# Unit 0 of a feature-crossing kernel: every x_b block selected by matmuls from x_a, none loaded; d stored earlier on SP, passes reordered

## The reference

```python
for Wk, bk in zip([W0, W1, W2], [b0, b1, b2]):
    z = jnp.einsum('bid,bjd->bdij', base, curr)
    curr = jnp.einsum('bdij,ijh->bhd', z, Wk) + bk[None, :, None]
    logit.append(curr)
pooled = jnp.sum(jnp.concatenate(logit, axis=1), axis=-1)
out = pooled @ lin_w + lin_b
```

## Time and profile before

| | us |
|---|---|
| median of 3 runs | 180.6 (180.23 to 180.7) |
| the profiled execution, own time | 180.91 |
| its span (first to last instruction) | 179.1 |
| PE busy | 173.1 (97%) |
| DVE busy | 153.1 (85%) |
| ACT busy | 72.9 (41%) |
| POOL busy | 11.9 (7%) |

### The profile page before, as it was taken

One profiled execution on the slowest core, in us unless ns is written; L12 is line 12 of the kernel. 1 busy time (PEld: TensorE's weight loads), 2 busy tenths in 40 slices (PEclk: granted clock), 3 DMA queues, 4 the chain that ended last, 5 costly groups with the idle time before them and its releaser, 6 DMA issues.

```text
span 179.1 us, 2565 instructions
## 1 busy us (share of the span) xinstructions
PE 173.1 (97%) x800; PEld 118.0 (66%) x800; DVE 153.1 (85%) x141; ACT 72.9 (41%) x80; POOL 11.9 (7%) x20
## 2 busy tenths in 40 slices
PE   6799998999999999999999999999999999999995
PEld 1264665767777777777777777777777777777772
DVE  0799966299999999999999999999999999995012
ACT  2554900064643364426442654255424641450020
POOL 3251804000000000000000000000000000000000
DMA  5999844999879577847794778577857760000000
GB/s 159 400 413 399 268 111 115 407 419 408 264 236 328 140 231 231 327 141 231 231 328 138 225 232 264 188 220 226 284 171 225 232 202 0 0 0 4 0 0 0
DMA packets 12668, 37.59 MB, mean 210 GB/s; under 512 B 2548, under 2 KB 3668, under 8 KB 12660
## 3 DMA queue, kind: packets, MB, share of 16 engines
q1 hardware_dynamic: 11408, 36.39, 61.2%
q10 hardware_dynamic: 1252, 1.09, 2.3%
HBM read 36.40 MB, written 1.07 MB: 209 GB/s over the span
## 4 chain that ended last, share of the span: by engine, by line
PE 85%; DMA 6%; DVE 4%; SPq 2%; issue 1%; ACT 0%; DVEq 0%
PE q_ps L497 42%; PE c_ps L497 39%; DMA x_a<-xa 3%; DVE xb_z L262 2%; DMA pair_sb<-d_dram 1%; SPq L172 1%; DMA d_dram<-w_d 1%; PE q_ps L562 1%; PE q_ps L506 1%; PE c_ps L541 1%; SPq L166 1%; PE c_ps L636 1%; PE q_ps L541 1%; PE c_ps L640 0%; DVE w_post L283 0%
## 5 line engine op out<-in xcount | busy, mean ns | idle before, releaser
L366 ACT ACTIVATE z_high<-xb_z 126x1024 fp32r<-126x1024 f32 x56 | 59.2, 1061 | 81.6 <-DVE xb_z L262 77.6
L269 DVE TENSOR_TENSOR z_low<-xb_z,z_high 126x1024 fp32r<-126x1024 f32 x56 | 68.7, 1231 | 0.5 <-ACT z_high L366 0.4
L262 DVE TENSOR_TENSOR xb_z<-x_a,xb_z 126x1024 f32<-126x1024 f32 x50 | 61.3, 1226 | 3.7 <-DMA xb_z<-xw 3.7
L497 PE MATMUL c_ps<-z_high,wc_high 126*101 126x512 f32 x112 | 35.4, 397 | 0.3 <-DVE z_low L269 0.3
L497 PE MATMUL c_ps<-z_high,wc_low 126*101 126x512 f32 x112 | 35.0, 394 | 0.0
L497 PE MATMUL c_ps<-z_low,wc_high 126*101 126x512 f32 x112 | 35.0, 394 | 0.0
L497 PE MATMUL q_ps<-z_high,wq_high 126*101 126x512 f32 x108 | 34.0, 396 | 0.9 <-DVE wq_low L312 0.9
L497 PE MATMUL q_ps<-z_high,wq_low 126*101 126x512 f32 x108 | 33.8, 394 | 0.0
L497 PE MATMUL q_ps<-z_low,wq_high 126*101 126x512 f32 x108 | 33.7, 393 | 0.0
L497 PEld LDWEIGHTS c_ps<-z_high,wc_high 126*101 126x101 f32 x112 | 18.2, 165 | 8.8 <-ACT z_high L366 1.0
L497 PEld LDWEIGHTS c_ps<-z_high,wc_low 126*101 126x101 f32 x112 | 18.5, 165 | 7.5
(11 more groups left out here) (58 smaller groups left out, 61.5 us busy)
## 6 DMA issues: line engine op xcount, KB each, us to landing
xb_z<-xw SPq DMA_DIRECT2D x50, 512.0 KB, 4.4
x_a<-xa SPq DMA_DIRECT2D x7, 512.0 KB, 5.1
w_post<-w1x SPq DMA_DIRECT2D x4, 512.0 KB, 8.7
w_d<-w2h SPq DMA_DIRECT2D x4, 404.0 KB, 6.3
pair_sb<-w_pairs SPq DMA_DIRECT2D x3, 202.0 KB, 9.9
xb_z<-xw ACTq DMA_DIRECT2D x2, 256.0 KB, 4.6
x_a<-xa SPq DMA_DIRECT2D x2, 256.0 KB, 4.7
d_dram<-w_d SPq DMA_DIRECT2D x2, 189.4 KB, 3.7
```

Source lines behind the costliest of these rows:

```text
L262: nc.vector.tensor_tensor(xb_z[0:K, c, :], x_a[0:K, u % 2, :], x_b, ALU.mult).then_inc(z_done, 1)
L269: nc.vector.tensor_tensor(z_low[0:K, m % SLOTS, :], xb_z[0:K, c, :], z_high[0:K, m % SLOTS, :].bitcast(fp32), ALU.subtract).then_inc(low_d ...
L366: nc.scalar.activation(z_high[0:K, m % SLOTS, :], xb_z[0:K, m % C, :], ACT.Copy).then_inc(high_done, 1)
L497: last = nc.tensor.matmul(ps[0:J, h * B:(h + 1) * B], w[0:K, c * J:(c + 1) * J], z[0:K, slot, h * B:(h + 1) * B], start=(c == 0 and k == 0 ...
```

## The change

`SELECTED` is 6: chunk 6 is selected as well, and chunk 0 by two selections of half the columns (`select_first`, `form_first`), so no x_b of unit 0 is loaded: the two 256 KB loads on ACT's queue and SP's last load (512 KB) go. Chunk 0's selection goes to `c1_ps[0]`; the order of the first instructions on PE, DVE and ACT is written anew; the warm-up loop runs 10 times, not 14. Two of the ten stores of d move from ACT to SP, one from SP to ACT. In `c1_chunk` and `q_chunk` the pass with the low weights is last, and the waits for `z_low` and for the low weights stand right ahead of the passes that use them.

```diff
-SELECTED = 5
+SELECTED = 6
-WARM = 14
+WARM = 10
-        sel_ps = (q_ps[0], c1_ps[1])
+        sel_ps = (c1_ps[0],) + (c1_ps[1], q_ps[0]) * (SELECTED // 2 + 1)
...
@@ sync: stores of d
             store_d(sp, 1, LEFT + UPPER_AT[0], 0, 2 * GI, (DR - DB, DR))
+            store_d(sp, 0, LEFT + F, 0, RIGHT, (32, DR))
+            store_d(sp, 1, LEFT - 2 * GI, 0, 2 * GI, (0, 32))
             sp.wait_ge(dgroup_copied_dve, 1)
             store_d(sp, 0, LEFT + 2 * GI, 2 * GI, GI, (0, DB))
             store_d(sp, 1, LEFT + UPPER_AT[2], 2 * GI, GI, (DR - DB, DR))
-            store_d(sp, 1, 0, 3 * GI - (LEFT - 2 * GI), LEFT - 2 * GI, (0, 32))
...
@@ vector
-            form_first(0, xa_first, xb_first)
             split_x(0)
-            form_first(1, xa_loaded[0], xb_loaded[0]).then_inc(z_done, 1)
             split_x(1)
-            split(0, 0)
+            form_first(0).then_inc(formed_first, 1)
+            form_first(1).then_inc(z_done, 1)
             form(0, 1)
             form(0, 2)
+            split(0, 0)
+            form(0, 3)
             split(0, 1)
+            form(0, 4)
             split(0, 2)
-            form(0, 3)
-            form(0, 4)
-            form(0, 5)
             copy_d(2)
             split(0, 3)
+            form(0, 5)
+            split(0, 4)
             form(0, 6)
-            for m in range(4, C):
-                split(0, m)
+            split(0, 5)
+            split(0, 6)
...
@@ scalar
-            load_first_xb(0, xb_first)
-            load_first_xb(1, xb_loaded[0])
...
+            act.wait_ge(formed_first, 1)
             round_high(0, 0)
             cast_w0(0)
+            act.wait_ge(const_done, 1)
+            nc.scalar.activation(const_sb[:, :], const_ps, ...).then_inc(const_copied, 1)
             round_high(0, 1)
-            round_high(0, 2)
             act.wait_ge(v_multiplied, 1)
             nc.scalar.activation(v_rows[:, :], v_ps, ACT.Copy).then_inc(v_rows_copied, 1)
-            act.wait_ge(const_done, 1)
+            round_high(0, 2)
...
-            act.wait_ge(dgroup_copied, 3)
-            store_d(act, 0, LEFT + F, 0, RIGHT, (32, DR))
-            store_d(act, 1, LEFT - 2 * GI, 0, 2 * GI, (0, 32))
             round_high(0, 3)
             copy_d(3)
+            act.wait_ge(dgroup_copied_dve, 1)
+            store_d(act, 1, 0, 3 * GI - (LEFT - 2 * GI), LEFT - 2 * GI, (0, 32))
+            round_high(0, 4)
             cast_w0(2)
             cast_w0(3)
...
@@ tensor
+            def chunk_pass(ps, w, z, m, first, last):
+                c, slot = m % C, m % SLOTS
+                for h in range(2):
+                    end = nc.tensor.matmul(ps[0:J, h * B:(h + 1) * B], w[0:K, c * J:(c + 1) * J],
+                                           z[0:K, slot, h * B:(h + 1) * B],
+                                           start=(c == 0 and first), stop=(c == C - 1 and last))
+                return end
...
             def c1_chunk(it, m):
...
+                chunk_pass(c1_ps[u % 2], wc_high, z_high, m, True, False)
+                pe.wait_ge(low_done, it * BODY + (m + 1))
+                chunk_pass(c1_ps[u % 2], wc_high, z_low, m, False, False)
+                if m in WC_CUTS[:-1]:
+                    pe.wait_ge(wc_ready, WC_CUTS.index(m) + 1)
+                last = chunk_pass(c1_ps[u % 2], wc_low, z_high, m, False, True)
...
             def q_chunk(it, m):
                 if m in PREP_CUTS[:2]:
+                    pe.wait_ge(wq_highs, PREP_CUTS.index(m) + 1)
...
+                chunk_pass(q_ps[u % 2], wq_high, z_high, m, True, False)
+                chunk_pass(q_ps[u % 2], wq_high, z_low, m, False, False)
...
-            c1_chunk(0, 0)
...
+            turn_v()
             c1_chunk(0, 0)
...
             d_group(3)
-            for m in range(1, C):
+            c1_chunk(0, 1)
+            select_xb(6)
+            for m in range(2, C):
                 c1_chunk(0, m)
```

More of the change, by code:

```diff
@@ L491, in _ @@
         def _(pe):
-            def chunk_products(ps, high, low, m):
+            def chunk_pass(ps, w, z, m, first, last):
                 c, slot = m % C, m % SLOTS
-                for k, (w, z) in enumerate(((high, z_high), (low, z_high), (high, z_low))):
-                    for h in range(2):
-                        last = nc.tensor.matmul(ps[0:J, h * B:(h + 1) * B], w[0:K, c * J:(c + 1) * J],
-                                                z[0:K, slot, h * B:(h + 1) * B],
-                                                start=(c == 0 and k == 0), stop=(c == C - 1 and k == 2))
-                return last
+                for h in range(2):
[3 more added lines that the diff above has]
+                return end
             def last_q(m, cols):
                 c, slot = m % C, m % SLOTS
-                for k, (w, z) in enumerate(((wq_high, z_high), (wq_low, z_high), (wq_high, z_low))):
+                for k, (w, z) in enumerate(((wq_high, z_high), (wq_high, z_low), (wq_low, z_high))):
                     last = nc.tensor.matmul(q_ps[1][0:J, cols], w[0:K, c * J:(c + 1) * J], z[0:K, slot, cols],
```

74 lines of the change are left out of this document (39 added, 35 removed).

## The result

| | before | after |
|---|---|---|
| median | 180.57 us (22 runs) | 179.61 us (22 runs) |
| ratio, with its 95% interval | | 0.9952 (0.9939 to 0.9965) |
| profiled execution: own time, span | 180.91, 179.1 | 180.35, 178.6 |
| a second profiled execution of each | 180.67, 178.8 | 179.61, 177.8 |
| a third of changed | | 179.51, 177.7 |

By the medians the kernel became 0.96 us faster. The ratio, 0.87 us, leaves out three slow executions (183.56, 182.99 and 181.88). The forecast was 2.0, and 179.61 lies just above the range's end of 179.6.

The account below looks back on a forecast made before the run. PE bounds the body, so q's start counts: 1.7 us earlier, plus the 0.27 wait less 0.05, in all 1.9 to 2.0. 180.91 - 2.0 = 178.9, less 0.3 to the median: 178.6 us; range 177.8 to 179.6.

Parts of the forecast that it names:

- the body and what q waits for: From q on, PE keeps its pace; q's first pass waits for wq_high alone, 0.4 us gained at its start.
- T: The moment at which the gathers ahead of q may go: 23.56 us before, forecast 22.25.
- The wait of 0.27: PE's wait for z_low at c1's chunk 7 in the body; it goes, counted as 0.27 less 0.05 us.
- every later load lands 1.28 earlier: In the head, without the first two removed loads, W2's last piece lands at 10.1 us and W1's at 15.9.
- the rate of one window: The head's transfers run at 411 GB/s, so the first two removed loads are worth 1.28 us.
- a long store: One store's issue in SP's row took 1.31 us before, not 0.42; if that comes again, T is 22.3.
- T by POOL: POOL's low weights and memset, behind ACT's casts of W0, end at 22.25 us and hold the gathers.
- T by the stores: SP issues d's stores 0.47 us apart, the last at 19.2; landing 2.19 later, T would be 21.4.
- the cover of v_sb: In the head, PE does c1's chunk 0, 1.4 us, until 13.05, while v_sb is made by 12.5.
- T stays late: Rival, 0.17: the long store pushes or POOL is held up twice; T 22.8 to 23.3, time 179.2 to 179.7 us.
- PE as the bound: Rival, 0.25: T below 21.9, so q begins when c1 is done, 26.5 or 26.2; time 178.0 to 178.3 us.
- The clock: Rival, 0.07: after ten warm-ups, head work to 17.5 us at half speed: 184 us; with half of that, 181.6.

Follow-up runs that it names:

- b_passes: The kernel before with only the new order of passes and its waits in c1 and q: 179.95 us, ratio 0.9968.
- a_passes: The changed kernel with the old order of passes and the old waits in c1 and q: 180.15 us, ratio 0.998 to the kernel before.
- a_bal: The changed kernel with the two stores of d that had gone to SP back on ACT: 180.07 us, ratio 0.9978 to the kernel before.
- a_both: The changed kernel with two d stores back on ACT and W0's last two casts ahead of ACT's last store and chunk 4's rounding: 179.76 us.
- a_best2_w: Changed with two loads on ACT's queue, W0's last casts earlier, c1's chunk 0 behind the third d group, and 14 warm-ups: 179.52 us, ratio 0.9946.
- a_loads_w: The changed kernel with the three removed loads put back as unused transfers and 14 warm-ups: 179.96 us, ratio 0.9964 to the kernel before.
- a_best1: The changed kernel with two loads on ACT's queue, two d stores back on ACT and W0's last casts earlier: 179.14 us, ratio 0.9902.
- b_warm10: The kernel before with 10 warm-up matmuls in place of 14: 183.17 us, ratio 1.0153.
- a_best2: Changed with two loads on ACT's queue, W0's last casts earlier, c1's chunk 0 behind the third d group, v_sb's copy before a rounding: 178.91 us.
- a_two: The changed kernel with the loads of the small constants and W0's first piece on ACT's queue, not SP's: 179.12 us, ratio 0.9926.
- the loads-back kernel: The changed kernel, ten warm-ups, with the three removed loads put back as transfers nobody uses: 180.93 us, ratio 1.004 to the kernel before.

## Why the prediction was wrong

**Right: the body and what q waits for.** q begins 4.63, 4.68 and 4.47 behind T; forecast 4.6. The stretch from q on is 0.2 to 0.3 shorter, forecast 0.22. Taken together, 0.5 to 0.6 by the two pass experiments, against 0.62. (The wait of 0.27 was only partly one: q's first matmul to c1's chunk 7 went from 9.87 to 9.76, and the rest came in the body behind it.) Two traces temper this. In that of b_passes the first gathers landed late, 2.87 behind their last issue for 2.56 and 2.68, and q began 4.90 behind T; in that of a_passes the old order cost at q's third chunk and not at its first. So the price of the order holds, by two experiments, and the place at which it is paid depends on when the gathers land.

**The step that failed first: "every later load lands 1.28 earlier".** W2's last piece was to land at 10.1 and landed at 11.37, 10.73 and 10.99, for 11.43 and 11.15 before, and by the runs with fourteen warm-ups the loads are worth 0.1 to 0.2 us of the time. Its first part did land 0.9 to 1.4 earlier; its last part, for which PE waits, fell behind. The bytes were gone, but the queue that carried them was a second one, and without it W2's packets took longer and the parts spread. The experiment with two loads on ACT's queue brought the rate back, and the landing fell to 9.44. Why one queue is slower here stays open. The forecast used the rate of one window, 9.3 to 12, for a stretch in which it had not been read.

This step alone accounts for most of the miss. All that follows on PE kept the forecast's distances: the first d group began 2.87, 2.88 and 2.89 behind W2's last piece (forecast 2.95), and c1's chunk 1 another 4.51 to 4.52 behind that (4.45). W2 was late by 1.27, 0.63 and 0.89. T, for which the working with a long store gave 22.3, was late against that by 1.4, 0.6 and 0.7, and q's first matmul against 26.85 by 1.48, 0.74 and 0.65. The 0.3 by which the forecast lowered its time from the profiled execution to a median is the rest of the 1.0, since the second trace of changed lies at the median itself.

**The second: "T by POOL", the case with 0.46.** The memset did end near the forecast (22.48 to 23.11, for 22.25), but T was at the stores in every trace. It was T by the stores that was too small, 21.4. Its working is otherwise sound: the copy of group 1 came 0.4 late in the second trace (the loads), and the rest, 1.1, is the long issue of one store, 1.71 for 0.42, less what the others saved. The forecast saw the 1.31 of before, had nothing to explain it, and took the usual 0.42. In the sum this was hidden: 22.25 by POOL, a bound that did not hold, is by luck the 22.3 that the stores give with a long issue. It was no accident of one trace: each of the eighteen traces of all these kernels has a fetch between 15.9 and 21.3 us, and in fifteen a store's issue of 0.8 to 1.7 us overlaps it. In a_bal and a_both, where SP was done early, the fetch came behind the issues and the last parts landed late instead, and in a_best2_w, where it fell between two stores, no issue was above 0.56. Against the fetch as the cause: issues of 0.84, 0.89, 0.83 and 0.99 stand in a_bal, a_both, a_loads_w and a_best1 without a fetch beside them, and one of 1.29 in b_warm10 began 1.07 ahead of its fetch. And behind 26 us, where loads are issued singly, twenty issues overlap a fetch in the eighteen traces, and eighteen of them took 0.33, like the others (the two left, 0.54 and 0.81). So a long issue is at most a matter of a fetch and a row of stores together. That the fetch has a part in it is inferred from the coincidence. No experiment moved the fetch itself, so this stays open, as does whose instructions it brings.

**A cost that the sum had in it: c1's chunk 0 ahead of the d groups.** The forecast called it the cover of v_sb and counted its 1.4 whole, so nothing of the miss comes from here; but it is dear. In a_loads_w, with the selections at 495 and 501 and then 392 to 398 ns, v_sb begins at 13.20 and the first d group at 14.18; in the kernel before these were 13.41 and 13.77. So d waited 0.6 longer behind v_sb than in before. With the chunk moved behind the third d group and v_sb's copy ahead of a rounding (a_best2), the first d group began at 11.80, for 12.88 with the two loads alone.

**The rivals.** "T stays late" names the long store and T from 22.8 on, and its time, 179.2 to 179.7, holds the result; it had 0.17. By the forecast's own 22.3 the long store alone doesn't bring T there; the late loads had to come to it, which it does not name. PE as the bound came with c1's chunk 0 moved, and in the one trace of a_passes. The clock did not do in the changed kernel what the rival feared. That fits the reason that was given: PE's idle stretch between warm-up and first selection is 0.20 to 0.39 there, for 0.73 to 1.05 before. (Its 184 should read 184.6 by its own terms, 180.6 + 6 - 2.) But it was nearer than 0.07 let one think. The same ten warm-ups with that stretch at 1.1 and 2.26 us cost 0.97 and 2.6, and the removal of the loads, worth next to nothing in bytes, is what keeps it short. Nor was the case free of it: the first trace lost 0.46 at two selections. The statement of the Trainium skill that was quoted (TensorE: Matmul & The Clock Gate, Part 1) holds here: the number of warm-ups that ran at the low level differs between executions of one kernel, 6 and 11 of fourteen in the two traces of before, 10, 7 and 9 of ten in the three of changed.

## What to carry to other kernels

When a load is removed, ask which queue it was in as well as how many bytes it had, and look at the last part of the loads behind it, not the first: here the transfers left behind moved 7% less from 1.5 to 9.5 us in one queue, and two loads of 248 and 103 kB moved to the idle queue brought 0.5 us. Before an experiment that puts one thing back is read as its price, compare the durations of single instructions in its trace: here three quarters or more of what looked like the price of a megabyte was TensorE's clock. And a long duration that stands once in a trace, at a place on the path, is to be priced as if it came again until a second trace says otherwise.

## What the runs showed of the hardware

- In the 4 us after 3.5 us the transfers moved 283 to 356 GB/s with SP's queue alone (three traces of changed), and 355 to 412 with ACT's queue used as well (before, loads put back, a_two), at a DMA share of 0.94 to 1.07.
- The parts of one load can land far apart. Of W2's last piece the last part came 1.0 to 2.4 us behind the first in the eight traces with the loads of changed, 0.7 to 1.0 in the kernel before and its variants, and 0.4 to 0.7 in the four with two loads on ACT's queue.
- A 16 KB instruction fetch in the head lasts 0.95 to 1.2 us. Its moment differs by 2.7 us between two executions of changed. In fifteen of eighteen traces a store that was issued beside it, in a row of stores, took 0.8 to 1.7 us to issue instead of 0.42; in a_bal and a_both it began behind the last issue, and the last parts landed 1 us late. Which causes which is not shown.
- The granted clock showed the low level where it had come back (0.50 and 0.66 in b_warm10) but not where it had not yet been left: 1.00 in the windows of the loads-back kernel in which selections took 628 ns for 395, and over ten warm-ups of 624 ns. There the durations tell, and the column does not.
